# One wait per PE instruction in the sorted edge steps of a graph network

## The chip, the cores and the metric

The kernel runs on one core of one Trainium2 chip. The metric is the device time of the whole program in microseconds. The kernel before takes 2650.18 us, the median of 3 runs (2649.66 to 2650.37).

## The reference

Four message-passing steps on a graph with 3125 nodes of 128 features and 50000 edges, then a final layer norm over the sum with the input. The edges come sorted by their target node. All tensors are fp32.

```python
edge_attr = swish(edge_attr_raw @ enc_W + enc_b)              # 50000 x 4 -> 50000 x 128
for _ in range(4):
    e_in = concatenate([edge_attr, x[src], x[dst]], axis=-1)  # 50000 x 384
    e_upd = layernorm(swish(e_in @ eW1 + eb1) @ eW2 + eb2, eg, ebeta)   # hidden width 256
    edge_attr = edge_attr + e_upd
    agg = segment_sum(edge_attr, dst, num_segments=3125)
    n_in = concatenate([x, agg], axis=-1)
    x = x + layernorm(swish(n_in @ nW1 + nb1) @ nW2 + nb2, ng, nbeta)
x = layernorm(x_in + x)
```

## The kernel before

The program is written by hand, engine by engine: each engine has its own instruction list, and order between engines comes from counting semaphores (`wait_ge` in front of an instruction, `then_inc` on one). For sorted edges the class `Fast` is used.

The 50000 edges are cut into G1 = 98 groups of GE = 512 edges (TPG = 4 tiles of 128). One step s (0 to 3) runs over its 98 groups and then does the node update. Groups are counted on through the steps, n = 98 s to 98 s + 97. Features that need precision are kept as two fp16 parts, high and low, so most products are three matmuls.

In one iteration n PE does, in this order:

- `hidden(n)`, the first layer, into the PSUM tile `ps_h(n % 2)`: L1595, 4 matmuls of 256 columns, adds the target node's part by a one-hot matrix `oht` from a window of the node table (`q_win`, semaphores q0 to q3); L1603, 16 matmuls of 128 columns, adds the gathered source rows (`rows`, fetched by GpSimd's indirect DMAs); L1615, 6 matmuls of 512 columns, multiplies the old edge state by the weights and raises "h".
- `turn(n + 1)` (steps 1 to 3): L1629, 8 transposes of the next group's stored state, raises "transposed". ACT copies them (L1789) and raises "eT", for which L1615 of the next group waits.
- `output(n - 1)`, the second layer, into `ps_v`: L1642 puts the bias down (in step 0 from the third group on ACT's copy L1752, "seed", does this), then L1647, 24 matmuls of 128 columns, six for each tile t; raises "v". It waits for "hl", the low part of the hidden values, DVE's L1843.
- `turn_back(n - 4)` (step 0 alone): L1659, 8 matmuls.
- `node_sums(n - 7)`: in step 0 L1674, 4 matmuls, then L1678, 8 matmuls, which sum a group's edges into a window of 128 nodes in PSUM, `ps_a`; raises "sum". There is one `ps_a`, so it has to wait till DVE has added the window of the group before to `agg` (L1923, in step 0 L1920: "added"); it also waits for the group's new state ("el", DVE's L1904) and in step 0 for the one-hot matrix ("oh" of the init semaphores).
- `encode(n + 2)` (step 0 alone): L1384, one fp32 matmul that encodes the raw edge attributes.

ACT does for each group two swish passes over `ps_h` (L1743, L1744, 1024 columns), the copy L1789, four squares with sums (L1765), and the high part of the new state (L1779). DVE works in slots, one a group. Slot n is: the window add of group n - 8 ("added"), in step 0 the one-hot matrices of group n + 2 (L1475, L1476) and a low part (L1484), then L1843 of group n ("hl"), then a reciprocal root over pairs of groups (L297 to L305; seven to nine of its eleven small operations lie in odd slots, the rest in even ones), the scaling of group n - 4 (L1884, L1895), the low part of group n - 6 (L1904, "el"), and the gain L1853 of group n - 1 ("gu"). In odd slots L1904 comes behind the scaling, in even ones ahead of it.

SP loads the stored state (L1514, semaphores st0 to st7), the one-hot matrices (L1519, oh0 to oh3, which waits for "h" of group n - 4 and "sum" of group n - 12), stores the new state (L1532) and loads the window of the node table (L1526, L1527). GpSimd issues four gathers a group (L1572); the first waits for L1603 of group n - 4, the third for "v" of group n - 5.

Of the kernel before, what the change touches and what calls it, by code (L numbers as in the profile page):

```python
# [32 lines left out]
TPG = 4  # L33
GE = TPG * P
G1 = -(-E // GE)
# [9 lines left out]
R = 4  # L45
# [4 lines left out]
LAG = 4  # L50
# [12 lines left out]
def build_program(nc, attr_t, x_in, src_in, dst_in, attr_in, enc_W, enc_b, eW1, eb1, eW2, eb2, eg, ebeta,  # L63
                  nW1, nb1, nW2, nb2, ng, nbeta, out):
    ctx = ExitStack()
    with ctx:
# [1254 lines left out]
        class Fast:  # L1321
# [52 lines left out]
            def encodes(self, pe):  # L1374

                def encode(n):
                    if n >= G1:
                        return
                    pe.wait_ge(Z(f"at{n % R}"), 16 * self.ring(n))
                    if n == 1:  # L1380
                        pe.wait_ge(Z("enc"), n)
                    if n >= 4:
                        pe.wait_ge(self.S("gu"), n - 3)
                    pe.matmul(self.encoded(n), enc5[:, :], at5[n % R][0:RAW + 1, :],  # L1384
                              start=True, stop=True, skip_group_check=True).then_inc(Z("encm"), 1)

                return encode
# [189 lines left out]
            def pe(self, pe, s, node):  # L1577
# [3 lines left out]
                def hidden(n):  # L1581

                    k, k2 = n % R, n % 2
                    both_hot = oht[n % R12]
                    if s:
                        pe.wait_ge(S(f"oh{k}"), 16 * self.ring(n))
                    else:
                        pe.wait_ge(Z("oht"), n + 1)
                    pe.wait_ge(S(f"q{k}"), 32 * self.ring(n))
                    if n >= 2:  # L1590
                        pe.wait_ge(S("hl"), n - 1)
                    fence(pe)
                    for half in range(2):
                        for h in range(2):
                            pe.matmul(ps_h(k2)[:, half, h * HALF_E:(h + 1) * HALF_E],  # L1595
                                      q_win[k][:, h * H + half * D:h * H + half * D + D],
                                      both_hot[:, h * HALF_E:(h + 1) * HALF_E],
                                      start=h == 0, stop=False, skip_group_check=True)
                    pe.wait_ge(*self.gathered(n))
                    for t in range(TPG):  # L1600
                        for half in range(2):
                            for p in range(2):
                                x = pe.matmul(ps_h(k2)[:, half, t * P:(t + 1) * P],  # L1603
                                              rows[k][:, t, p * H + half * D:p * H + half * D + D], ident16[:, :],
                                              start=False, stop=False, skip_group_check=True)
                    x.then_inc(S("src"), 1)
                    if s:
                        pe.wait_ge(S("eT"), n - G1 + 1)
                    else:
                        pe.wait_ge(Z("lo"), n + 1)  # L1610
                    old = eT[k2] if s else turned_in[n % RE]
                    for half in range(2):
                        cols = slice(half * D, (half + 1) * D)
                        for w, p in ((w1_hi, 0), (w1_hi, 1), (w1_lo, 0)):
                            x = pe.matmul(ps_h(k2)[:, half, :], w[:, cols], old[:, p, :],  # L1615
                                          start=False, stop=w is w1_lo, skip_group_check=True)
                    x.then_inc(S("h"), 1)

                def turn(n):
# [1 line left out]
                    if not first <= n <= last or s == 0:  # L1621
                        return
                    pe.wait_ge(*self.loaded(n))
                    if n > G1:
                        pe.wait_ge(S("eT"), n - G1)
                    for p in range(2):
                        for t in range(TPG):
                            m = p * TPG + t
                            x = pe.transpose(ps_t[:, m * P:(m + 1) * P], st_in[n % RE][:, p, t * P:(t + 1) * P], ident16[:, :])  # L1629
                    x.then_inc(S("transposed"), 1)  # L1630

                def output(n):

                    k2 = n % 2
                    if s == 0 and n >= 2:
                        pe.wait_ge(S("seed"), n - 1)
                    else:
                        if n >= 2:
                            pe.wait_ge(S("gu"), n - 1)
                        if s == 0:  # L1640
# [1 line left out]
                        pe.matmul(ps_v(k2), ones16[:, :], v_bias[:, :], start=True, stop=False, skip_group_check=True)  # L1642
                    pe.wait_ge(S("hl"), n + 1)
                    for t in range(TPG):
                        for half in range(2):
                            for h, w in ((hh, w2_hi), (hh, w2_lo), (hl, w2_hi)):
                                x = pe.matmul(ps_v(k2)[:, t * P:(t + 1) * P], h[k2][:, half, t * P:(t + 1) * P], w[:, half, :],  # L1647
# [3 lines left out]
                def turn_back(n):  # L1651
# [3 lines left out]
                    if n:  # L1655
                        pe.wait_ge(S("new"), n)
                    for t in range(TPG):
                        for p in range(2):
                            x = pe.matmul(ps_e[:, t * P:(t + 1) * P], turned_in[n % RE][:, p, t * P:(t + 1) * P], ident16[:, :],  # L1659
                                          start=t == 0 and p == 0, stop=p == 1, skip_group_check=True)  # L1660
# [2 lines left out]
                def node_sums(n):  # L1663
# [1 line left out]
                    if n < first:  # L1665
                        return
                    pe.wait_ge(S("el"), n + 1)
                    if n:
                        pe.wait_ge(S("added"), n)
                    if s == 0:  # L1670
                        pe.wait_ge(Z("oh"), n + 1)
                    fence(pe)
                    for t in range(TPG if s == 0 else 0):
                        pe.matmul(ps_a[:, P:2 * P], ones16[:, :], oh[n % R12][:, t * P:(t + 1) * P],  # L1674
                                  start=t == 0, stop=t == TPG - 1, skip_group_check=True)
# [740 lines left out]
```

## Time and profile before

| | us |
|---|---|
| median of 3 runs | 2650.18 |
| the profiled execution, span | 3010.4 |
| step 0, first to last L1595 | 93.2 to 744.7 |
| steps 1, 2, 3, first to last L1595 | 843.9 to 1475.5, 1572.4 to 2202.8, 2299.6 to 2929.2 |
| PE busy | 2519.3 (84%) |
| DVE busy | 2296.5 (76%) |
| ACT busy | 1995.8 (66%) |
| POOL busy | 1569.8 (52%) |

The profiled execution's own span is 360 us longer than the median of the runs without a profile. Times in the rows are microseconds from the start of the span.
### The profile page before, as it was taken

The numbers are of one execution on the slowest core, as the hardware profiler recorded it, in microseconds if no ns is written. First come the engines' busy times: TensorE is split into PE (matmuls) and PEld (weight loads), VectorE is DVE, ScalarE is ACT, GpSimd is POOL, SyncE is SP. The second block draws the span as 40 slices with busy tenths as digits, with TensorE's granted clock in tenths as the row PEclk, the third lists the DMA queues.
The fourth block names the chain that finished last, engine by engine and source line by source line (L and its number), as shares of the span: only waits on it lengthen the run. The fifth ranks groups of instructions, "written<-read, shape, count | busy, mean of one in ns | idle before, by whom it ended". The sixth has DMA issues, their size and how long they took to land.

```text
span 3010.4 us, 83926 instructions
## 1 busy us (share of the span) xinstructions
PE 2519.3 (84%) x27990; PEld 1876.1 (62%) x27990; DVE 2296.5 (76%) x6586; ACT 1995.8 (66%) x5343; POOL 1569.8 (52%) x1581
## 2 busy tenths in 40 slices
PE   3699999999858888888876888888885888888885
PEld 1467776677536666666645666666663666666664
DVE  5499999899637787777854787777773688877787
ACT  2478787777437777777635777777753777777774
POOL 0566666664056666666215666666603666666640
PEclk9799999999989999999999999999998999999998
DMA  3556666564256666667445666666734555555540
GB/s 95 158 180 178 185 184 186 177 184 147 93 151 206 209 207 207 207 209 210 129 137 156 209 210 208 206 207 210 209 101 138 161 168 168 168 166 167 167 134 22
DMA packets 380881, 512.91 MB, mean 170 GB/s; under 512 B 57676, under 2 KB 254418, under 8 KB 380440
## 3 DMA queue, kind: packets, MB, share of 16 engines
q1 hardware_dynamic: 305176, 301.81, 32.0%
q0 software_dynamic: 75264, 205.62, 24.0%
q8 instruction: 228, 3.74, 0.5%
q14 instruction: 213, 1.74, 0.2%
HBM read 389.35 MB, written 117.85 MB: 168 GB/s over the span
## 4 chain that ended last, share of the span: by engine, by line
PE 76%; issue 11%; ACT 4%; another core or an unknown queue 4%; DVE 3%; DMA 1%; POOL 0%; DVEq 0%; ACTq 0%; SPq 0%; POOLq 0%
PE psum L1647 17%; PE psum L1615 16%; PE psum L1603 13%; PE psum L1678 6%; PE psum L1595 6%; PE psum L1629 4%; PE psum L1384 3%; PE psum L2081 3%; PE psum L1642 2%; PE psum L2120 2%; PE psum L2094 1%; PE psum L1659 1%; ACT arena L1765 1%; ACT psum L1744 1%
## 5 line engine op out<-in xcount | busy, mean ns | idle before, releaser
L1572 POOL DMA_INDIRECT arena<-node_tables,idx_all x1568 | 1567.2, 999 | 1345.2 <-remote 528.1
L1843 DVE SCALAR_TENSOR_TENSOR arena<-psum,arena 128x1024 f16<-128x1024 f32 x392 | 479.6, 1223 | 520.6 <-issue 370.9
L1743 ACT ACTIVATE arena<-psum 128x1024 f16<-128x1024 f32 x392 | 401.1, 1023 | 576.4 <-PE psum L1615 443.9
L1647 PE MATMUL psum<-w_hi,arena 128*128 128x128 f16 x6272 | 604.1, 219 | 37.5 <-ACT psum L1752 21.9
L1603 PE MATMUL psum<-ident,arena 128*128 128x128 f16 x6272 | 481.4, 220 | 165.9 <-issue 160.5
L1647 PE MATMUL psum<-w_lo,arena 128*128 128x128 f16 x3136 | 553.1, 219 | 3.8 <-issue 3.1
L1647 PEld LDWEIGHTS psum<-w_hi,arena 128*128 128x128 f16 x6272 | 498.2, 98 | 75.8 <-ACT psum L1752 40.3
L1603 PEld LDWEIGHTS psum<-ident,arena 128*128 128x128 f16 x6272 | 390.4, 98 | 242.1 <-issue 222.5
L1615 PE MATMUL psum<-arena,w_hi 128*128 128x512 f16 x1568 | 473.3, 384 | 41.3 <-ACT arena L1789 39.8
L1765 ACT ACTIVATE arena<-psum 128x128 f32<-128x128 f32 x1568 | 412.5, 279 | 100.9 <-remote 79.2
L1744 ACT ACTIVATE psum<-psum 128x1024 f32<-128x1024 f32 x392 | 398.9, 1018 | 0.0
L1884 DVE SCALAR_TENSOR_TENSOR arena<-arena 128x128 f32<-128x128 f32 x1176 | 366.8, 343 | 3.0
L1647 PEld LDWEIGHTS psum<-w_lo,arena 128*128 128x128 f16 x3136 | 307.0, 98 | 46.7 <-issue 5.6
L1765 ACT ACTIVATION_READ_ACCUMULATOR arena<-psum 128x1 f32 x1568 | 327.9, 209 | 0.0
L1789 ACT COPY arena<-psum 128x1024 f16<-128x1024 f16 x294 | 298.9, 1017 | 42.6 <-remote 38.3
L1678 PE MATMUL psum<-arena 128*128 128x128 fp8e4 x3136 | 241.6, 219 | 96.2 <-issue 87.9
L1615 PE MATMUL psum<-arena,w_lo 128*128 128x512 f16 x784 | 300.4, 383 | 0.0
L1853 DVE TENSOR_TENSOR arena<-psum,g_row 128x512 f32<-128x512 f32 x392 | 267.5, 682 | 9.9 <-ACT arena L1765 6.8
L1904 DVE SCALAR_TENSOR_TENSOR arena<-arena 128x512 f16<-128x512 f32 x392 | 267.8, 683 | 0.0
L1595 PE MATMUL psum<-arena 128*128 128x256 fp8e4 x1568 | 241.3, 275 | 31.4 <-issue 23.5
L1678 PEld LDWEIGHTS psum<-arena 128*128 128x128 f16 x3136 | 188.5, 98 | 126.6 <-issue 125.6
L1779 ACT CAST arena<-arena 128x512 f16<-128x512 f32 x392 | 248.7, 635 | 0.0
(174 smaller groups left out, 3258.7 us busy)
## 6 DMA issues: line engine op xcount, KB each, us to landing
state<-arena SPq DMA_DIRECT2D x294, 256.0 KB
arena<-state SPq DMA_DIRECT2D x294, 256.0 KB
arena<-node_tables SPq DMA_DIRECT2D x784, 64.0 KB
arena<-matrices SPq DMA_DIRECT2D x294, 128.0 KB
node_tables<-arena SPq DMA_DIRECT2D x100, 256.0 KB, 2.2
arena<-node_tables,idx_all POOLq DMA_INDIRECT x1568
arena<-rel_rows SPq DMA_DIRECT2D x98, 128.0 KB
matrices<-arena SPq DMA_DIRECT2D x98, 128.0 KB
```

What stands on the lines that cost most here:

```text
L1572: pool.indirect_dma_start(out=rows[n % R][:, t, :], out_offset=None, in_=p_table, in_offset=bass.IndirectOffsetOnAxis(ap=idx_all[:, n % G1 ...
L1595: pe.matmul(ps_h(k2)[:, half, h * HALF_E:(h + 1) * HALF_E], q_win[k][:, h * H + half * D:h * H + half * D + D], both_hot[:, h * HALF_E:(h ...
L1603: x = pe.matmul(ps_h(k2)[:, half, t * P:(t + 1) * P], rows[k][:, t, p * H + half * D:p * H + half * D + D], ident16[:, :], start=False, st ...
L1615: x = pe.matmul(ps_h(k2)[:, half, :], w[:, cols], old[:, p, :], start=False, stop=w is w1_lo, skip_group_check=True)
L1647: x = pe.matmul(ps_v(k2)[:, t * P:(t + 1) * P], h[k2][:, half, t * P:(t + 1) * P], w[:, half, :], start=False, stop=half == 1 and h is hl, ...
L1678: x = pe.matmul(ps_a[:, 0:P], st_out[n % R][:, p, t * P:(t + 1) * P], oh[n % R12][:, t * P:(t + 1) * P], start=t == 0 and p == 0, stop=t = ...
L1743: act.activation(hh[k2], ps_h(k2), ACT.Silu).then_inc(S("hh"), 1)
L1744: act.activation(ps_h(k2), ps_h(k2), ACT.Silu).then_inc(S("h32"), 1)
L1765: x = act.activation(sq[k2][:, t * P:(t + 1) * P], ps_v(k2)[:, t * P:(t + 1) * P], ACT.Square, accum_out=nv[pair][:, m:m + 1])
L1789: act.copy(eT[n % 2], ps_t[:, :].rearrange("c (k e) -> c k e", k=2)).then_inc(S("eT"), 1)
L1843: dve.scalar_tensor_tensor(hl[k2], ps_h(k2), 1.0, hh[k2], ALU.mult, ALU.subtract).then_inc(S("hl"), 1)
L1884: x = dve.scalar_tensor_tensor(e_new[k][:, cols], gu[k][:, cols], rs[pair][:, m:m + 1], old, ALU.mult, ALU.add)
```

## The change

Six places of `Fast`, all in what PE does in the edge steps:

- `hidden`: the fence is gone. The waits for the one-hot matrix (in steps 1 to 3 "oh k", in step 0 "oht") and for "hl" of group n - 2 in front of L1595 are gone; only the window's wait "q k" stays (in step 0 "oht" for the first two groups). In step 0 from the fourth group on, the second half of L1615 waits for "seed" of the group whose output follows.
- `turn`: its wait for "eT" is gone. Before its fifth transpose it now waits for the one-hot matrix "oh" of the group that it turns.
- `output`: in step 0 "seed" is waited for here only at the last group; before tile t = 1 stands the wait for "oht" of the group after next (step 0), and before tile t = 3, the last, the wait for "added", with the same count for which `node_sums` of the same iteration waited. It stands from the eighth group of a step on.
- `turn_back`: before t = 2 stands the wait for the raw attributes that the `encode` of this iteration reads.
- `node_sums`: the fence is gone and so is "oh"; "added" is waited for here only at the step's edges (its first group and its last ones).
- `encode`: waits for its attributes itself only for the first six groups.

```diff
-                    pe.wait_ge(Z(f"at{n % R}"), 16 * self.ring(n))
+                    if n < LAG + 2:
+                        pe.wait_ge(Z(f"at{n % R}"), 16 * self.ring(n))
...
-                    if s:
-                        pe.wait_ge(S(f"oh{k}"), 16 * self.ring(n))
-                    else:
+                    if s == 0 and n < 2:
                         pe.wait_ge(Z("oht"), n + 1)
                     pe.wait_ge(S(f"q{k}"), 32 * self.ring(n))
-                    if n >= 2:
-                        pe.wait_ge(S("hl"), n - 1)
-                    fence(pe)
...
                         cols = slice(half * D, (half + 1) * D)
+                        if half and s == 0 and n >= 3:
+                            pe.wait_ge(S("seed"), n - 2)
...
-                    if n > G1:
-                        pe.wait_ge(S("eT"), n - G1)
                     for p in range(2):
+                        if p:
+                            pe.wait_ge(S(f"oh{n % R}"), 16 * self.ring(n))
...
-                    if s == 0 and n >= 2:
+                    if s == 0 and n == last:
                         pe.wait_ge(S("seed"), n - 1)
-                    else:
+                    if s or n < 2:
...
                     for t in range(TPG):
+                        if t == 1 and s == 0 and n + 2 <= last:
+                            pe.wait_ge(Z("oht"), n + 3)
+                        if t == TPG - 1 and n - 6 > first:
+                            pe.wait_ge(S("added"), n - 6)
...
                     for t in range(TPG):
+                        if t == 2 and n + LAG + 2 < G1:
+                            pe.wait_ge(Z(f"at{(n + LAG + 2) % R}"), 16 * self.ring(n + LAG + 2))
...
                     pe.wait_ge(S("el"), n + 1)
-                    if n:
+                    if n == first and n or n + 6 > last:
                         pe.wait_ge(S("added"), n)
-                    if s == 0:
-                        pe.wait_ge(Z("oh"), n + 1)
-                    fence(pe)
```

## Rows read from the trace of the kernel before

**Rows 1.** The page: busy time of each engine, and the chain that ended last.
```profile
PE 2519.3 (84%) x27990; PEld 1876.1 (62%) x27990; DVE 2296.5 (76%) x6586; ACT 1995.8 (66%) x5343; POOL 1569.8 (52%) x1581
...
PE 76%; issue 11%; ACT 4%; another core or an unknown queue 4%; DVE 3%; DMA 1%; POOL 0%; DVEq 0%; ACTq 0%; SPq 0%; POOLq 0%
```

**Rows 2.** Line L1595, steps 0 and 1: ns min/median/max, first and last start.
```profile
L1595 PE MATMUL psum<-arena x392: 272/273/421, 93.2 to 744.7; 128*128 128x256 fp8e4 x196
L1595 PE MATMUL psum<-arena x392: 269/273/417, 843.9 to 1475.5; 128*128 128x256 fp8e4 x196
```

**Rows 3.** Groups of PE instructions, step 1: busy us, mean ns | idle before.
```profile
L1603 PE MATMUL psum<-ident,arena 128*128 128x128 f16 x1552 | 123.9, 220 | 53.8 <-issue 53.6
...
L1678 PE MATMUL psum<-arena 128*128 128x128 fp8e4 x717 | 55.5, 218 | 26.5 <-issue 26.5
```

**Rows 4.** Timeline in the middle of step 1: L1615's end and ACT's L1743.
```profile
1117.89 0.38 PE L1615 MATMUL psum<-arena,w_lo 128*128 128x512 f16 x1
1119.63 1.02 ACT L1743 ACTIVATE arena<-psum 128x1024 f16<-128x1024 f32 x1 [1.55 <-PE psum L1615]
```

**Rows 5.** Timeline of the last groups of step 1.
```profile
1464.33 0.60 PE L1595 MATMUL psum<-arena 128*128 128x256 fp8e4 x4
...
1467.62 0.22 PE L1647 MATMUL psum<-w_hi,arena 128*128 128x128 f16 x1
...
1468.90 0.22 PE L1647 MATMUL psum<-w_hi,arena 128*128 128x128 f16 x1
...
1469.10 0.28 DVE L1923 TENSOR_TENSOR agg_deg<-agg_deg,psum 128x128 f32 x1
1469.30 1.22 DVE L1843 SCALAR_TENSOR_TENSOR arena<-psum,arena 128x1024 f16<-128x1024 f32 x1
1469.48 0.61 PE L1678 MATMUL psum<-arena 128*128 128x128 fp8e4 x8 [0.36 <-issue]
1469.92 0.60 PE L1595 MATMUL psum<-arena 128*128 128x256 fp8e4 x4
...
1472.33 0.38 PE L1615 MATMUL psum<-arena,w_lo 128*128 128x512 f16 x1
...
1472.75 1.02 ACT L1743 ACTIVATE arena<-psum 128x1024 f16<-128x1024 f32 x1 [1.17 <-PE psum L1615]
...
1474.39 0.28 DVE L1923 TENSOR_TENSOR agg_deg<-agg_deg,psum 128x128 f32 x1
...
1474.49 0.22 PE L1647 MATMUL psum<-w_hi,arena 128*128 128x128 f16 x1
...
1474.77 0.61 PE L1678 MATMUL psum<-arena 128*128 128x128 fp8e4 x8
1474.77 1.22 DVE L1843 SCALAR_TENSOR_TENSOR arena<-psum,arena 128x1024 f16<-128x1024 f32 x1
1475.21 0.60 PE L1595 MATMUL psum<-arena 128*128 128x256 fp8e4 x4
```

**Rows 6.** The fences on PE's sequencer, whole run: ns min/median/max, starts.
```profile
L288 PEldq EVENT_SEMAPHORE  x784: 51/51/6122, 93.1 to 2966.3; - x196
```

**Rows 7.** Timeline in the middle of step 0: L1595, and DVE's window add.
```profile
305.18 0.61 PE L1595 MATMUL psum<-arena 128*128 128x256 fp8e4 x4
311.89 0.61 PE L1595 MATMUL psum<-arena 128*128 128x256 fp8e4 x4
318.13 0.61 PE L1595 MATMUL psum<-arena 128*128 128x256 fp8e4 x4
...
308.38 0.41 DVE L1920 TENSOR_TENSOR agg_deg<-agg_deg,psum 128x256 f32 x1
```

**Rows 8.** Step 0: the seed, L1647 behind it; then all its waits in sum.
```profile
307.64 0.59 ACT L1752 COPY psum<-v_row 128x512 f32<-128x512 f32 x1
...
308.28 0.23 PE L1647 MATMUL psum<-w_hi,arena 128*128 128x128 f16 x1 [0.30 <-ACT psum L1752]
...
PE psum L1647 <- ACT psum L1752: 21.9, 24, 1.8
```

## The prediction

> **What bounds the kernel now.** I read the page first: the engine with most busy time is PE, 84% of the span, and the chain that ended last runs over PE for 76% of it [rows 1]. Then the time by stage: the loop over the groups takes 651.5 us in step 0 and 631.6 us in step 1 [rows 2], and within 2 us of that in steps 2 and 3. In step 1 that is 631.6 / 97 = 6.51 us a group, while PE's own work for a group, from L1678 at 1469.48 to the end of L1647 (last start 1474.49, free again at 1474.55), is 5.07 us without a gap [rows 5].
>
> The profiled run is 360 us longer than the median of 2650.18 us, so first it must be known what the recording adds. In mid-loop ACT starts L1743 at 1119.63, although the last L1615 matmul that it waits for is shown from 1117.89 to 1118.27: 1.36 us late [rows 4]. In the last groups of step 1 the same handover takes 0.04 us (1472.33 + 0.38 to 1472.75), and the groups take 5.59 and 5.29 us (L1595 at 1464.33, 1469.92, 1475.21) [rows 5]. In mid-loop PE also idles inside L1603, where no line waits: 53.6 us of "issue" in step 1 [rows 3]; the last two groups have none of it. I take these two groups as the kernel without the recording's load. The Trainium skill (Perfetto Trace Analysis, Tensor Engine Instruction) says that the end shown for a matmul is an estimate and that the semaphore's propagation is not in the record; the trace agrees in so far as an increment can come well behind the end shown.
>
> The check on that choice: with 5.44 instead of 6.51 us, the 291 groups of steps 1 to 3 lose 311 us; with 6.24 us in step 0, which PE fills without a gap from 311.89 to 318.13, instead of 651.5 / 97 = 6.72 [rows 2, 7], another 46 us go. 3010.4 - 311 - 46 = 2653 us, against 2650.18 measured.
>
> So what makes a group 5.44 us when PE's work is 5.07? In [rows 5] PE is through with L1647 at 1468.96 and starts L1678 only at 1469.48; DVE's window add L1923 ends at 1469.38. In the next group L1923 ends at 1474.67 and L1678 starts at 1474.77. Both times it is 0.10 us behind the add. So "added" releases PE, and not "el", which L1904 raises earlier in the same slot of DVE. From the add it is a loop over three engines: 0.10 us, L1678 to the end of L1615 (1469.48 to 1472.71), ACT's L1743 and L1744, DVE's L1843 at 1474.77: 5.39 us after the add's end. DVE needs 5.37 us from L1843 to the end of its next window add in this slot, an odd one (1469.30 to 1474.67); even slots are shorter. Two groups therefore take at least 5.39 + 5.37 = 10.76 us, 5.38 us each. That is what binds, not PE's 5.07 us.
>
> **The change part by part.** *Standalone waits.* A fence or a second wait is an instruction of PE's sequencer, 51 ns when it doesn't block [rows 6]; four a group go in steps 1 to 3, six in step 0. Those behind L1678 have its 0.44 us and the matmuls of L1595 as cover, the one of `turn` has L1603: 0. Without any cover it would be 4 x 0.051 x 294 + 6 x 0.051 x 98 = 90 us. The fence in front of L1678 is different: there the matmul starts 0.10 us behind the add. A wait attached to the weight load takes 0.05 us: ACT's L1752 ends at 308.23, L1647 starts at 308.28 [rows 8]. That is a gain of 0.05 us on the loop.
>
> *The covered waits*, "hl" of group n-2 in `hidden` and "eT" in `turn`: PE's queue has already waited for both values, in `output` and `hidden`. 0.
>
> *"added"* moves from in front of L1678 to t = 3 of `output`. The count is the same, but six L1647 matmuls now stand behind it. L1647 repeats every (1468.90 - 1467.62) / 23 = 0.056 us, so 6 x 0.056 = 0.33 us of PE's work moves from before the add's end to behind it. Is PE held there? t = 3 would start at 1467.62 + 18 x 0.056 = 1468.63 and at 1474.49 - 5 x 0.056 = 1474.21, against add ends of 1469.38 and 1474.67: held for 0.75 and 0.46 us, so all of the 0.33 us goes onto the loop [rows 5]. Queued behind it are the rest of `output`, for which ACT's squares wait (they stand behind L1744 and L1789 in ACT's list, and that is their cover), then `node_sums` and `hidden` and through it ACT and DVE. Bounds: 0 if the add were always early, the 0.33 us in every group if the loop were one slot long.
>
> *"oh"* moves to the middle of `turn(n+1)`, some 2.4 us ahead of its old place. The load waits for L1615 of four groups before, so about three groups less 2.4 us remain to it, 13 us; nothing in the rows shows PE waiting for it. 0.
>
> *"seed"* in step 0 moves ahead of the second half of L1615, three matmuls or 0.65 us earlier. L1647 is held by it 24 times, 21.9 us in sum [rows 8]. In the recorded run its new place would come at 305.18 + 0.44 + 0.89 + 0.65 = 307.16, before the seed's end at 308.23 [rows 7, 8]; that lateness is of the size of the recording's 1.36 us, so without it the seed is about in time: 0, with an upper bound of 24 x 0.65 = 16 us. *"oht", "at"*: nothing waits for them in the rows, 0. *"added"* in step 0: L1920 ends at 308.79, and PE is at t = 3 only at 308.28 + 1.01 = 309.29: 0 [rows 7, 8].
>
> **The sum.** On the loop +0.33 - 0.05 = +0.28 us for two groups, 0.14 us each: 5.52 instead of 5.38. It acts where the new wait exists and a later `hidden` follows it: 89 groups in each of three steps, 267. 267 x 0.14 = 37 us. On the profiled execution cleared of the recording that is 2653 + 37 = 2690, on the median 2650 + 37 = 2687 us. I forecast 2687, 1.4% slower. The profiled span won't show this: in mid-loop the recording holds it, and four to six records of some 140 a group go, so it may even fall (2940 to 3030 us).
>
> **The rivals.**
> A, the forecast: the "added" loop binds. For it: 0.10 us behind the add in both undisturbed groups, and the check of 2653 us. Against: only two groups a step show it. Its price lies between +18 us (half the groups held) and 0.33 x 267 = +89 us.
> B, faster: what costs is that the sequencer stands in the fence while PE's queue runs dry; with every wait attached it reads on. The Trainium skill (Advanced Engine Details and Errata, Sequencer Loop) says this much, that an engine instruction waits in the queue while later ones are read. From rows: the idle time before L1678 is 0.36 us in one undisturbed group and 1474.77 - 1474.55 = 0.22 us in the next [rows 5]; were it the fence's own, 0.29 x 294 = 85 us would go, and all standalone instructions exposed give 90 us: 2560. A half of it is 2605. For it: 26.5 us of "issue" before L1678 in step 1 [rows 3]. Against: that idle time ends 0.10 us behind L1923, which an attached wait sits out too.
> C, the same: in the run without a profile most groups are uneven, as step 0's 6.71 beside 6.24 us [rows 7], and the earlier wait meets an add already done: 2645 to 2655.
> D, slower in another place: the seed holds L1615 in step 0 and so delays `hidden` itself, up to +16 us, beside A.
>
> **How the numbers follow.** A, with D on top, 0.60 (2668 to 2740, mostly under 2715); B 0.22 (2560 to 2644); C 0.18. About 0.2%, 5 us, is what a measurement of this kernel can tell from no change. Faster 0.22, same 0.17, slower 0.61. A's own range is 2668 to 2715; to leave out no more than 2 in 10 it takes in C and the nearer half of B: 2610 to 2715.
>
> **What would show it.** In the profile of the changed kernel: no rows of L288, L1591 or L1625 on PE inside the loops. In the last two groups of a step the idle time sits inside L1647, ahead of its last six matmuls, and ends 0.05 us behind L1923; L1678 follows without a gap, and the L1595 distances are 0.1 to 0.3 us longer than 5.59 and 5.29. For B they would be about 5.1 to 5.2 us. The forecast is wrong if in undisturbed groups the add ends before PE is at t = 3, or if the idle time at L1603 is in the unprofiled run too and not only in the record.

## The result and the profile after

The changed kernel takes 2712.89 us, the median of 4 runs (2710.74 to 2717.46), beside 2649.92 us for the kernel before in the same rounds. The ratio is 1.0241, 95% interval [1.0228, 1.0253]: 63 us slower, where 37 were forecast.

The page of after, the rows that answer to [rows 1]:
```profile
PE 2428.5 (90%) x27990; PEld 1868.7 (69%) x27990; DVE 2289.2 (84%) x6586; ACT 1983.8 (73%) x5343; POOL 1627.4 (60%) x1581
```
The span of this profiled execution is 2711.4 us, what the runs take without a profile, so nothing has to be cleared away. The shares of busy time went up although the kernel got slower, because the span of before was stretched by 360 us. Its busy microseconds are stretched too: PE has the same 27990 matmuls in both and 2519.3 us there against 2428.5 here. So neither can be compared with [rows 1].

The line that was L1595 is L1591 now, in steps 0 and 1, as [rows 2]:
```profile
L1591 PE MATMUL psum<-arena x392: 272/273/418, 93.4 to 702.7; 128*128 128x256 fp8e4 x196
...
L1591 PE MATMUL psum<-arena x392: 272/273/422, 805.1 to 1347.5; 128*128 128x256 fp8e4 x196
```
Step 1 takes 542.4 us, 5.59 us a group. I had taken 5.44 us for before, and to its loop of 5.38 us the forecast added 0.14 to get 5.52. (These rows run to the last of the last group's four matmuls; to its first it is 542.1 us, as in the table below.)

Groups of PE instructions in step 1 (busy us, mean ns | idle before), as [rows 3]; L1649 is the old L1647, L1679 the old L1678:
```profile
L1649 PE MATMUL psum<-w_hi,arena 128*128 128x128 f16 x1536 | 153.0, 220 | 37.8 <-DVE agg_deg L1924 37.5
...
L1599 PE MATMUL psum<-ident,arena 128*128 128x128 f16 x1552 | 103.4, 220 | 3.7 <-DMA arena<-node_tables,idx_all 3.7
...
L1679 PE MATMUL psum<-arena 128*128 128x128 fp8e4 x717 | 54.7, 219 | 0.0
```
The idle time has left the window sums and sits inside the second layer, and what ends it is the window add. L1599, the old L1603, has lost its 53.6 us of "issue".

Timeline of the last groups of step 1, as [rows 5]:
```profile
1335.01 0.28 DVE L1924 TENSOR_TENSOR agg_deg<-agg_deg,psum 128x128 f32 x1
...
1335.34 0.23 PE L1649 MATMUL psum<-w_hi,arena 128*128 128x128 f16 x1 [0.85 <-DVE agg_deg L1924]
...
1335.69 0.61 PE L1679 MATMUL psum<-arena 128*128 128x128 fp8e4 x8
1336.13 0.60 PE L1591 MATMUL psum<-arena 128*128 128x256 fp8e4 x4
...
1338.55 0.38 PE L1613 MATMUL psum<-arena,w_lo 128*128 128x512 f16 x1
1338.96 1.02 ACT L1744 ACTIVATE arena<-psum 128x1024 f16<-128x1024 f32 x1 [1.42 <-PE psum L1613]
...
1341.00 1.23 DVE L1844 SCALAR_TENSOR_TENSOR arena<-psum,arena 128x1024 f16<-128x1024 f32 x1 [1.13 <-issue]
1341.21 0.60 PE L1591 MATMUL psum<-arena 128*128 128x256 fp8e4 x4
...
1346.10 0.27 DVE L1924 TENSOR_TENSOR agg_deg<-agg_deg,psum 128x128 f32 x1
...
1347.22 0.60 PE L1591 MATMUL psum<-arena 128*128 128x256 fp8e4 x4
```
The loop of the forecast can be followed row by row. The add ends at 1335.29, the held matmul starts 0.05 us later, six matmuls pass before L1679 at 1335.69, L1613 ends at 1338.93, ACT takes over at 1338.96, L1844 starts at 1341.00, 5.71 us behind the add, and the next long slot's add ends at 1346.37, 5.37 us later. The group distances are 5.08 and 6.01 us, 11.09 for two, where [rows 5] have 5.59 and 5.29. One group in two isn't held at all: the six matmuls add to every second group, as the two-slot loop has it. The sign that I had named, both distances 0.1 to 0.3 us longer than 5.59 and 5.29, was too narrow: one is shorter, and only the sum of the two is longer.

In mid-loop the slot on DVE is a little longer:
```profile
1005.57 1.22 DVE L1844 SCALAR_TENSOR_TENSOR arena<-psum,arena 128x1024 f16<-128x1024 f32 x1 [1.06 <-issue]
1006.71 0.23 DVE L297 TENSOR_SCALAR arena<-arena 128x8 f32<-128x8 f32 x1
...
1010.74 0.28 DVE L1924 TENSOR_TENSOR agg_deg<-agg_deg,psum 128x128 f32 x1
...
1011.07 0.23 PE L1649 MATMUL psum<-w_hi,arena 128*128 128x128 f16 x1 [0.84 <-DVE agg_deg L1924]
```
From L1844 to the add's end are 5.45 us here (1011.02 - 1005.57), and 5.46 as the median of the long slots of steps 1 to 3. With 5.71 that gives 11.17 us for two groups, the measured 5.59 each. Nearly all of the 0.08 us more than at the step's end is in one operation, L297, the root's first, which takes 0.16 us there (at 1342.14) and 0.23 here.

### The profile page after: what moved, and what is told of

Its sections match the earlier page's. It is cut to its first block, busy times and chain, and to the rows that moved or that the text cites. A ratio compares the mean times of both kernels' runs of the same rounds, so it can differ in the third digit from the quotient of the medians.

```text
span 2711.4 us, 82205 instructions
## 1 busy us (share of the span) xinstructions
PE 2428.5 (90%) x27990; PEld 1868.7 (69%) x27990; DVE 2289.2 (84%) x6586; ACT 1983.8 (73%) x5343; POOL 1627.4 (60%) x1581
## 4 chain that ended last, share of the span: by engine, by line
PE 68%; issue 11%; DVE 8%; ACT 7%; POOL 3%; DMA 2%; DVEq 1%; ACTq 0%; SPq 0%; POOLq 0%
PE psum L1613 17%; PE psum L1649 12%; PE psum L1599 12%; PE psum L1679 6%; PE psum L1591 6%; ACT psum L1745 5%; PE psum L1385 4%; POOL arena L1573 3%; PE psum L2082 2%; PE psum L2121 2%; PE psum L1627 2%; DVE agg_deg L1924 2%; PE psum L1663 2%; PE psum L2095 2%; DVE arena L1885 1%
## 5 line engine op out<-in xcount | busy, mean ns | idle before, releaser
L1573 POOL DMA_INDIRECT arena<-node_tables,idx_all x1568 | 1624.8, 1036 | 985.1 <-DMA node_tables<-arena 421.2
L1649 PE MATMUL psum<-w_hi,arena 128*128 128x128 f16 x6272 | 624.2, 220 | 129.6 <-DVE agg_deg L1924 119.7
L1844 DVE SCALAR_TENSOR_TENSOR arena<-psum,arena 128x1024 f16<-128x1024 f32 x392 | 478.3, 1220 | 236.2 <-issue 138.6
L1649 PEld LDWEIGHTS psum<-w_hi,arena 128*128 128x128 f16 x6272 | 502.1, 98 | 175.6 <-DVE agg_deg L1924 147.5
L1649 PE MATMUL psum<-w_lo,arena 128*128 128x128 f16 x3136 | 556.9, 220 | 0.0
L1613 PE MATMUL psum<-arena,w_hi 128*128 128x512 f16 x1568 | 470.4, 382 | 1.3 <-ACT arena L1790 1.3
L1599 PE MATMUL psum<-ident,arena 128*128 128x128 f16 x6272 | 417.8, 220 | 14.4 <-DMA arena<-node_tables,idx_all 14.3
L1599 PEld LDWEIGHTS psum<-ident,arena 128*128 128x128 f16 x6272 | 384.5, 98 | 28.5 <-DMA arena<-node_tables,idx_all 19.6
L1766 ACT ACTIVATION_READ_ACCUMULATOR arena<-psum 128x1 f32 x1568 | 339.3, 216 | 0.0
L1649 PEld LDWEIGHTS psum<-w_lo,arena 128*128 128x128 f16 x3136 | 307.2, 98 | 45.8
L1613 PE MATMUL psum<-arena,w_lo 128*128 128x512 f16 x784 | 299.3, 382 | 0.0
L1591 PE MATMUL psum<-arena 128*128 128x256 fp8e4 x1568 | 238.6, 275 | 26.0 <-DMA arena<-node_tables 26.0
L1679 PE MATMUL psum<-arena 128*128 128x128 fp8e4 x3136 | 240.9, 220 | 5.9 <-DVE agg_deg L1924 5.9
L1896 DVE SCALAR_TENSOR_TENSOR arena<-arena 128x512 f32<-128x512 f32 x294 | 205.2, 698 | 5.1
```

The costliest lines, as they stand in the source:

```text
L1573: pool.indirect_dma_start(out=rows[n % R][:, t, :], out_offset=None, in_=p_table, in_offset=bass.IndirectOffsetOnAxis(ap=idx_all[:, n % G1 ...
L1591: pe.matmul(ps_h(k2)[:, half, h * HALF_E:(h + 1) * HALF_E], q_win[k][:, h * H + half * D:h * H + half * D + D], both_hot[:, h * HALF_E:(h ...
L1599: x = pe.matmul(ps_h(k2)[:, half, t * P:(t + 1) * P], rows[k][:, t, p * H + half * D:p * H + half * D + D], ident16[:, :], start=False, st ...
L1679: x = pe.matmul(ps_a[:, 0:P], st_out[n % R][:, p, t * P:(t + 1) * P], oh[n % R12][:, t * P:(t + 1) * P], start=t == 0 and p == 0, stop=t = ...
L1766: x = act.activation(sq[k2][:, t * P:(t + 1) * P], ps_v(k2)[:, t * P:(t + 1) * P], ACT.Square, accum_out=nv[pair][:, m:m + 1])
L1844: dve.scalar_tensor_tensor(hl[k2], ps_h(k2), 1.0, hh[k2], ALU.mult, ALU.subtract).then_inc(S("hl"), 1)
```

## The experiments

Times are medians; the ratio is to the kernel before in the same rounds (2653.2 us for the first four, 2647.6 for e5 to e8, 2650.8 for the last four). "Step 1" is from the first group's first matmul of L1595 to the last group's. "Release" is the median time from an add's end to the matmul that it holds, and "to low" from the add's end to the L1843 that hangs on it, both over steps 1 to 3 of the trace; where the early adds scatter it (e6, e9 to e12), "to low" is the tenth percentile.

| kernel | us | ratio [95%] | step 1 | a group | release | to low |
|---|---|---|---|---|---|---|
| after | 2712.9 | 1.0241 [1.0228, 1.0253] | 542.1 | 5.59 | 0.057 | 5.71 |
| e1_added_back | 2658.9 | 1.0028 [1.0017, 1.0039] | 528.9 | 5.45 | 0.147 | 5.45 |
| e2_added_alone | 2719.2 | 1.0251 [1.0234, 1.0268] | 542.3 | 5.59 | 0.057 | 5.71 |
| e3_no_fence | 2663.5 | 1.0038 [1.0024, 1.0052] | 529.2 | 5.46 | 0.146 | 5.45 |
| e4_seed_back | 2715.2 | 1.0236 [1.0219, 1.0253] | 542.0 | 5.59 | 0.057 | 5.71 |
| e5_added_t1 | 2836.1 | 1.0708 [1.0690, 1.0725] | 573.9 | 5.92 | 0.057 | 6.38 |
| e6_early_add_before | 2625.8 | 0.9910 [0.9893, 0.9926] | 517.3 | 5.33 | 0.101 | 5.40 |
| e7_early_add_after | 2670.6 | 1.0080 [1.0063, 1.0097] | 530.1 | 5.47 | 0.057 | 5.71 |
| e8_added_only | 2645.8 | 0.9991 [0.9981, 1.0001] | 524.5 | 5.41 | 0.058 | 5.38 |
| e9_added_only_early | 2622.4 | 0.9893 [0.9876, 0.9909] | 515.0 | 5.31 | 0.057 | 5.37 |
| e10_load_first | 2626.2 | 0.9904 [0.9888, 0.9921] | 519.5 | 5.36 | 0.102 | 5.41 |
| e11_load_first_added_only | 2627.2 | 0.9911 [0.9894, 0.9927] | 518.7 | 5.35 | 0.058 | 5.38 |
| e12_short_gain | 2625.1 | 0.9908 [0.9892, 0.9925] | 519.3 | 5.35 | 0.102 | 5.41 |

**e1_added_back**: the changed kernel with "added" waited for in `node_sums` again.
```diff
-                        if t == TPG - 1 and n - 6 > first:
-                            pe.wait_ge(S("added"), n - 6)
...
-                    if n == first and n or n + 6 > last:
+                    if n:
                         pe.wait_ge(S("added"), n)
```

> The changed kernel with one thing undone: the wait for added stands in front of L1678's matmuls again, at every group, and no longer at t = 3 of output. All else stays as changed: no fences, seed, oh, oht and at at their new places. Theory L (the loop DVE window add, PE, ACT, DVE binds, and the six second-layer matmuls behind the moved wait are what was added to it): all or nearly all of the 63 us go back, 2645 to 2658 us. Rival S (a good part comes from seed in step 0, or from the other moved waits): 2665 us or more. Rival F (the fences did some good, for instance by holding PE's sequencer back): stays near 2700.

Measured 2658.9 us, 1 us above the expected upper end: 54 of the 63 us are back by this wait alone. All else of the change stays in, without the gain that rival B gave it; it is even 0.28% slower than before.

**e2_added_alone**: the mirror of it, the kernel before with its fences and only this wait moved.
```diff
+                        if t == TPG - 1 and n - 6 > first:
+                            pe.wait_ge(S("added"), n - 6)
...
-                    if n:
+                    if n == first and n or n + 6 > last:
                         pe.wait_ge(S("added"), n)
```

> The kernel before with one part of the change alone: added is waited for at t = 3 of output instead of in the fence of node_sums. Both fences and every other wait stay as before. Theory L: the loop gets the 0.33 us and keeps the fence's other waits, 2695 to 2715 us. Rivals S and F: the move alone costs at most a third of the 63 us, under 2672.

Measured 2719.2 us, 4 above the expected upper end: the whole loss and a little more, with the same step of 542.3 us. The place of one wait is shown to be the cause, by putting it in and by taking it out.

**e3_no_fence**: before, without fences and covered waits; "added" stays in `node_sums`, behind "el".
```diff
-                    if n >= 2:
-                        pe.wait_ge(S("hl"), n - 1)
-                    fence(pe)
...
-                    if n > G1:
-                        pe.wait_ge(S("eT"), n - G1)
...
-                    if n:
-                        pe.wait_ge(S("added"), n)
                     if s == 0:
                         pe.wait_ge(Z("oh"), n + 1)
-                    fence(pe)
+                    if n:
+                        pe.wait_ge(S("added"), n)
```

> The kernel before without the two fence increments and without the two covered waits (hl in hidden, eT in turn); all other waits stay where they were, so a second wait is still an instruction of its own. Theory L: standalone instructions are covered and an attached added is some 0.05 us quicker over a loop of two groups, so 2640 to 2650 us. Were the standalone instructions worth their 51 ns each on PE (2 fences, 1 or 2 waits a group), 2600 to 2620. On the record: if the fences are what makes the profiled execution of the kernel before 360 us longer than its unprofiled time, this one's span is within 30 us of its time; if it is the number of recorded instructions, it stays above 2900.

Measured 2663.5 us, 10 slower and not up to 10 faster: a miss. The timeline of a held group, and the line of the waits of `node_sums` (L1666) on PE's sequencer:
```profile
1107.65 0.28 DVE L1917 TENSOR_TENSOR agg_deg<-agg_deg,psum 128x128 f32 x1
...
1108.05 0.46 PEld L1672 LDWEIGHTS psum<-arena 128*128 128x128 f16 x8 [0.72 <-issue]
1108.08 0.61 PE L1672 MATMUL psum<-arena 128*128 128x128 fp8e4 x8 [0.58 <-DVE agg_deg L1917]
```
```profile
L1666 PEldq EVENT_SEMAPHORE  x391: 51/51/51, 144.7 to 2619.7; - x196
```
The matmul starts 0.15 us behind the add's end, where the fence of before needs 0.10 [rows 5]. 0.046 us more on a loop of two groups is 0.023 a group; over the 264 groups of steps 1 to 3 in which "added" is waited for that is 6 us, more than half of the 10.

**e4_seed_back**: the changed kernel with "seed" waited for in `output` again.
```diff
-                        if half and s == 0 and n >= 3:
-                            pe.wait_ge(S("seed"), n - 2)
...
-                    if s == 0 and n == last:
+                    if s == 0 and n >= 2:
                         pe.wait_ge(S("seed"), n - 1)
```

> The changed kernel with the seed wait of step 0 back in output, in front of the second layer, instead of ahead of the second half of L1613. Theory L: seed is in time at either place, 2708 to 2716 us. Rival S: up to 16 us of the 63 are its, 2697 to 2705.

Measured 2715.2 us beside 2712.9: step 0 takes 611.4 us with it back and 609.0 without. Its ratio and after's lie within each other's intervals. Moving the seed costs nothing that can be measured; rival D's addition is out.

**e5_added_t1**: three times the dose. "added" stands before t = 1, 18 matmuls ahead of the end and not 6; "oht" changes places with it.
```diff
-                        if t == 1 and s == 0 and n + 2 <= last:
+                        if t == TPG - 1 and s == 0 and n + 2 <= last:
                             pe.wait_ge(Z("oht"), n + 3)
-                        if t == TPG - 1 and n - 6 > first:
+                        if t == 1 and n - 6 > first:
                             pe.wait_ge(S("added"), n - 6)
```

> The changed kernel with added waited for at t = 1 of output instead of t = 3 (oht in step 0 goes to t = 3 in exchange): eighteen second-layer matmuls stand behind the wait instead of six, 0.67 us more of PE's work. Theory L: the loop of two groups grows from 11.17 to 11.84 us, 5.92 us a group, over 267 groups +89 us on 2713: 2790 to 2815 us. Were the 63 us a cost of having a wait in the middle of output at all (a bubble at the wait), and not of what stands behind it, it would stay at 2705 to 2725.

Measured 2836.1 us, 21 above the expected upper end. PE's waits, the first for steps 1 to 3, the second for step 0 (us, times, longest):
```profile
PE psum L1649 <- DVE agg_deg L1924: 218.9, 159, 3.6
PE psum L1649 <- DVE agg_deg L1921: 27.0, 46, 3.3
```
"To low" goes from 5.71 to 6.38 us, 0.67 for 12 matmuls, 0.056 each, exactly the price of the forecast. The loops of steps 1 to 3 take 98 us more than after's together, which alone would be inside the expected range. In 132 pairs of groups the matmuls make 88 of them, and L297, 0.30 us here and 0.25 in after (medians), some 7. The other 25 us come from step 0, 634.2 us beside 609.0, where the add holds PE more often and longer than in after.

**e8_added_only**: e1 with "el" waited for only at a step's first group, so that "added" is the only wait and stands on the load.
```diff
-                    pe.wait_ge(S("el"), n + 1)
+                    if n == first:
+                        pe.wait_ge(S("el"), n + 1)
```

> The changed kernel with added back in front of L1678, as in the first of these experiments, and without the wait for el wherever added covers it (DVE raises el of group n in an earlier slot than the added that node_sums(n) waits for). So added is the only wait there and stands on the weight load itself. In the first experiment it stood on an instruction of the sequencer and L1678 began 0.147 us behind the add, against 0.101 behind the fence of the kernel before and 0.057 where it stands on the load at t = 3. Theory L with that delay as a term of the loop: 0.05 to 0.09 us less on a loop of two groups than there, 2645 to 2653 us. If the delay does not matter, the same as there, 2656 to 2662.

Measured 2645.8 us, in the expected range. In a held group:
```profile
962.62 0.28 DVE L1923 TENSOR_TENSOR agg_deg<-agg_deg,psum 128x128 f32 x1
...
962.95 0.62 PE L1678 MATMUL psum<-arena 128*128 128x128 fp8e4 x8 [0.43 <-DVE agg_deg L1923]
```
0.05 us behind the add. This is what the change could have been: one wait per instruction, without moving "added". It ends within 0.1% of before, so the 0.04 us saved against the fence is hardly to be seen, and it is some 10 us better than e1 (by the ratios, 0.9991 and 1.0028). Its loop closes in mid-loop too: 5.375 us to the low part and 5.38 to the end of the next long slot's add are 10.755 us, and the pairs of groups in steps 1 to 3 take 10.75 to 10.76 (median).

**e6_early_add_before** and **e7_early_add_after**: the remedy that the loop suggests, on either kernel. DVE does the window add ahead of the gain and not behind it. The same edit in both:
```diff
+                def early_add(m):
+                    if first <= m < last - 6:
+                        add_window(m, window(m))
...
-                    add_window(n - LAG - 4, window(n - LAG - 4))
+                    if n - LAG - 4 >= last - 6:
+                        add_window(n - LAG - 4, window(n - LAG - 4))
...
+                        early_add(n - LAG - 3)
                         gains(n - 1)
```

> The kernel before with DVE's window add moved ahead of the gain L1853 of the slot before (0.60 us earlier in DVE's list; the last seven groups of a step as before). PE's list is untouched, fences included. Theory L: the loop of two groups shrinks from 10.84 to 10.24 us, 5.12 us a group, where PE's own 5.07 us is nearly reached: -0.30 us over some 280 groups, 2560 to 2580 us. If the loop over added is not what binds the kernel before, nothing moves: 2645 to 2655.

> The changed kernel with the same earlier window add on DVE. Theory L: the loop shrinks from 11.17 to 10.57 us, 5.28 us a group, so 80 to 90 us below 2713: 2620 to 2640 us, slower than the same edit on the kernel before by about the same 50 to 60 us. If the change's cost were elsewhere on PE, the edit would give much less here than on the kernel before.

Measured 2625.8 and 2670.6 us: 22 and 42 us gained, right in direction, and well short of both expected ranges. DVE in a long slot of e6:
```profile
964.59 0.16 DVE L301 TENSOR_TENSOR arena<-arena 128x8 f32<-128x8 f32 x1
964.91 0.29 DVE L1923 TENSOR_TENSOR agg_deg<-agg_deg,psum 128x128 f32 x1 [0.16 <-issue]
965.11 0.68 DVE L1853 TENSOR_TENSOR arena<-psum,g_row 128x512 f32<-128x512 f32 x1
965.71 1.21 DVE L1843 SCALAR_TENSOR_TENSOR arena<-psum,arena 128x1024 f16<-128x1024 f32 x1
```
And the window from 850 to 1300 us (busy us of PE, its loads, DVE, ACT and POOL, then clock, DMA share, GB/s):
```profile
850.00:1300.00 450.00, 438.32 (x5694) 357.32 (x5692) 428.98 (x1230) 375.41 (x1018) 345.15 (x345) 1.00 0.82 250
```
The add came only 0.35 to 0.41 us earlier (5.08 instead of 5.43 us behind L1843 in long slots, 4.30 instead of 4.71 in short ones) and not the whole length of the gain: 0.16 us of idle time stands in front of it now. Two more things can be read here. DVE goes from L1853 to L1843 without a gap, and it is busy for 428.98 of the 450 us. So there were two theories for the missing gain: X, the loop from the add still binds; Y, DVE is full. The last four runs were made for that.

**e9_added_only_early**: e8's waits with the early add.

> The kernel of e8_added_only (no fences, no standalone waits in the loop, added attached to the first weight load of the window sums) with DVE's window add ahead of the gain, as in e6_early_add_before. e6 took 2625.8 us and not the 2570 expected; two reasons are in question. X: the loop from the add over PE and ACT to the low part still binds, 5.40 us behind the add plus 5.1 to 5.2 us on DVE to the add of the long slot, 5.25 to 5.30 us a group. Y: DVE itself is full (in the middle of step 1 of e6 it is busy 429 of 450 us). By X the shorter release here (5.38 instead of 5.40 us) brings 0.01 to 0.02 us a group, 3 to 5 us: 2620 to 2624. By Y it brings nothing: 2623 to 2628. This run alone won't tell them apart; it says whether the one-wait form and the early add go together.

Measured 2622.4 us, ratio 0.9893 [0.9876, 0.9909], where X expected 2620 to 2624. This is the shortest time of the study. It is below before beyond doubt, but the 3 us to e6 are within the spread of either (2619.6 to 2624.2 beside 2621.6 to 2627.1), and Y's 2623 to 2628 begins 1 us above: as expected, this run doesn't tell X from Y. The traces do: the median pair of groups takes 10.43 us in step 1 of e9 (5.375 to low and 5.05 on DVE) and 10.50 in e6 (5.40 and 5.08), so in most groups the add's loop binds.

**e12_short_gain**: e6 with half of the gain left out.
```diff
+                    T = TPG if n < LAG else 2
...
-                                      g_row[:, :].unsqueeze(1).to_broadcast([P, TPG, D]), ALU.mult).then_inc(S("gu"), 1)
+                                      g_row[:, :].unsqueeze(1).to_broadcast([P, T, D]), ALU.mult).then_inc(S("gu"), 1)
```

> e6_early_add_before with half of DVE's gain left out from the fifth group on (256 instead of 512 elements), a part of the computation that is missing in the result: 0.3 us less work of DVE a slot, behind the add and ahead of the next low part, so not on the add's loop. X (the add's loop binds) expects next to nothing: 2618 to 2626. Y (DVE is full) expects the group to fall from 5.33 to about 5.1 us, 50 to 70 us in all: 2560 to 2578.

Measured 2625.1 us, the time of e6 with 78 us less work on DVE (2225.2 instead of 2303.6 us busy). Y doesn't hold for the loop as a whole: DVE had idle time now (20.4 us ahead of L1843 from 850 to 1300 us), and no group got shorter by it. But that the time is the same is in part luck, since two things cancel. The first row is from e12, the second from e6:
```profile
959.04 0.35 DVE L297 TENSOR_SCALAR arena<-arena 128x8 f32<-128x8 f32 x1
```
```profile
895.61 0.82 DVE L2218 TENSOR_TENSOR x_all<-x_all,nbeta_row 128x640 f32<-128x640 f32 x1
```
L297 takes 0.35 us in e12 and 0.16 in e6, and it lies on the add's loop: the long slot takes 5.23 us instead of 5.08, and the median pair 10.64 instead of 10.50. In e6, on the other hand, DVE has one more operation, L2218 (`shift`, 0.82 us), in five slots of a step and one of its kind in five more of step 3. It stands between the gain and L1843 and puts that off, and one group behind it takes about 6.04 us and not 5.43: five times in steps 1 and 2, ten times in step 3. In e12, where the gain is shorter, no group at these places does. So here Y holds, for some 12 us of e6.

**e10_load_first**: e6 with the register load at the head of the slot.
```diff
+                held = {}
...
-                        add_window(m, window(m))
+                        add_window(m, held.pop(m))
...
+                    if first <= n - LAG - 3 < last - 6:
+                        held[n - LAG - 3] = window(n - LAG - 3)
```

> e6_early_add_before with one difference: the register that holds the window's column is loaded at the head of DVE's slot and not right in front of the add. In e6 the add of a long slot stands 0.16 us behind the last small operation of the root, with no wait that holds it; if that is the register load, the idle time goes. By X and by Y alike two groups get shorter by up to 0.16 us (X) or 0.33 us (Y, both slots), 0.08 to 0.16 us a group, 24 to 48 us in 291 groups: 2580 to 2603 us. If the 0.16 us is something else, the time stays at e6's 2625.

Measured 2626.2 us, no gain. PE's waits from 850 to 1300 us, in e6 and then in e10:
```profile
PE psum L1678 <- DVE agg_deg L1923: 5.2, 8, 0.8
PE psum L1678 <- issue: 4.7, 24, 0.3
PE psum L1603 <- DMA arena<-node_tables,idx_all: 0.3, 1, 0.3
```
```profile
PE psum L1603 <- DMA arena<-node_tables,idx_all: 12.1, 21, 1.5
PE psum L1678 <- DVE agg_deg L1923: 0.4, 2, 0.2
```
The edit did what it was made for: the idle time in front of the add is gone (L1904 at 961.62 and L1923 at 962.29 follow closely), and PE's wait for the add falls from 9.9 us to 0.4. Its place is taken at once by L1603, which waits for the gathered source rows, 12.1 us instead of 0.3. These rows count idle time only from the shown end of a matmul, 0.22 us behind its start. From start to start, over what the same two lines take when nothing holds them, PE lost 18.5 us in this window in e6, in 46 of 85 groups and all of it ahead of L1678; in e10 it lost 4.1 us there and 17.1 ahead of L1603. So neither X nor Y is the answer for e10; the gathers are the next limit, and they lie within a few microseconds of the add's.

**e11_load_first_added_only**: e10's DVE order with e8's waits.

> e10_load_first's order on DVE together with e8_added_only's waits on PE. By X 3 to 5 us below e10: 2576 to 2599. By Y, and if by then PE's own 5.07 us come near, the same as e10.

Measured 2627.2 us, the same as e10 and 5 us above e9. With the gathers in the lead a shorter release buys nothing. Over the whole run its L1599 (the old L1603) waits 60.4 us in 71 places, e9's 19.7 in 19.

What holds the gathers back is open. GpSimd is busy for 347 of the 450 us of that window in e10, the DMA engines for 0.83 of it, and its first gather of a group waits for L1603 of four groups before; no run separates these. A second window buffer for the sums, which might take the add off PE's path, wasn't tried: the program's tiles already use all eight parts of its PSUM tensor.

## Why the prediction came out as it did

Its direction and its mechanism were right, the size was 26 us short. The range holds the result by 2 us only, in part by luck: the 26 us are three terms that I had put at nothing.

**What bounds the kernel: right.** The two groups at a step's end were the kernel without the recording's load. e1, e3 and e8, whose records aren't stretched and which differ from before only in how PE waits, take 5.41 to 5.46 us a group beside the 5.44 assumed. e5 and e2 move the time through the "added" wait alone.

**The price of six matmuls: right.** 5.71 us from add to low against e8's 5.38, with the same 0.057 us of release: 0.33 us, as forecast. e5 gives the same 0.056 us a matmul for twelve more.

**Attached instead of fence: right in size.** 0.101 to 0.057 us, forecast 0.10 to 0.05. It takes effect only where nothing else stands beside it; with "el" still in front (e1, e3) the release grew to 0.147 us, and I hadn't priced that.

**DVE's part of the loop: a term put at nothing.** I had taken DVE's 5.37 us, read from one slot at a step's end, to be the same before and after. In e8, whose time is that of before, it is 5.38 in mid-loop, so as a base it was good. In after it is 5.46, in e5 5.52, and nearly all of the difference is L297. Its median is 0.16 us in before, e1, e3, e6 and e8 to e11, where "added" stands in front of L1678, 0.25 to 0.26 in after, e2 and e4 and 0.32 in e7, where it stands at t = 3, and 0.30 in e5. The place of the wait alone doesn't set it, for in e12 it is 0.35. Two groups therefore grow by 0.33 - 0.04 + 0.08 = 0.37 us and not by 0.28. The count of groups was right: the first nine distances of a step take as long in after as in e8 (5.53 and 5.51 us on average), the other 88 take 5.60 and 5.40. 264 x 0.185 = 49 us stand beside the 37 forecast. Why L297 gets longer stays open: GpSimd's gathers, which are silent at the step's end, are there in e8's mid-loop as well, and its L297 stays at 0.16.

**Two more terms forecast at nothing: they weren't.** After against e8: steps 1 to 3 take 53 us more, step 0 609.0 instead of 601.9, and all that lies outside the four loops 475.7 instead of 468.1 us. 53 + 7 + 8 = 68 is the whole difference of their spans (2711.4 - 2643.6). Of the 53, up to 6 are the release, by which e8 is quicker than before. The other two can be read in after's record, the first row of what L1649 waits for in step 0 (us, times), the second from the end of step 1:
```profile
  DVE agg_deg L1921: 6.8, 30
```
```profile
1357.51 0.29 PE L1649 MATMUL psum<-w_hi,arena 128*128 128x128 f16 x1 [2.97 <-DVE agg_deg L1924]
```
In step 0 I had argued that PE reaches t = 3 half a microsecond behind the add. On the stretched record that was so, but here the add holds L1649 30 times, 6.8 us in sum, and e8 has no such wait. At a step's end the last group's second layer is held too: PE starts its last matmul 10.8 us behind the last group's L1591 and not 7.4 as in e8, at the end of steps 1 to 3, and 11.2 instead of 8.2 in step 0. How much of these 3.0 to 3.4 us reaches the next step differs (0.4 to 3.1 us). e2 has the same 610.9 and 477.2 us, so both terms belong to "added".

**Covered waits, fences, "oh", "seed", "oht", "at" at 0: right**, as far as e1, e4 and e8 show them together. The standalone instructions had their cover.

**Rival B fell.** Fences gone and "added" in its place (e1, e3, e8) is between 0.1% faster and 0.4% slower, not 1.7 to 3.4% faster. The idle time before L1678 was not the fence's. The Trainium skill (Advanced Engine Details and Errata, Sequencer Loop) is not contradicted: instructions may well be queued behind a waiting one, though no row here shows the reading ahead itself. It just was not what ended the idle time; DVE's add did, 0.1 us before each start. **Rival C fell** as well: in after's record, which isn't stretched, the groups do alternate, 5.07 and about 6.10 us, but with the add late in one of two and not in few.

**The profiled span: wrong.** I forecast 2940 to 3030 us; it was 2711.4. I had taken the stretching for a property of the kernel under a profile, and it belonged to that one execution. All thirteen other profiled executions lie within 3 us of their own unprofiled counterparts, e2 and e6 with the fences and the 27990 matmuls of before among them. The sign that I named was the idle time at L1603, 53.6 us of "issue" in step 1: in all of them no "issue" is left there, and the line's idle time is 4 to 7 us (18 in e10 and e11), put down to the gathers.

## What to carry to other kernels

A wait costs more the earlier it stands: every instruction between the new place and the old one goes onto the loop that the wait closes, here six matmuls, 0.33 us, in every second group. Before a wait is moved "to where there is room for it", find who raises it and when; if the engine already idles for it, leave it where it is and drop or cover the other conditions instead (e8), or make the raiser earlier (e6, e9). A loop's length is to be taken from many of its turns in the middle of a kernel's own record, and a change can lengthen an instruction that it doesn't touch (L297 here); if the span of a profiled run isn't the unprofiled time, its total must not be taken as the base for the next kernel.

## What the runs showed of the hardware

The time from the end of DVE's add to PE's start depends on where the wait stands, with almost no scatter: 0.057 us when it is the only condition and attached to the weight load (some 155 to 160 held groups of steps 1 to 3 each in after, e2 and e8, tenth to ninetieth percentile within 0.002), 0.101 us when it ends a standalone sequencer instruction in front of a load without a condition (144 in e6), and 0.147 us when a load with a condition of its own, raised earlier, follows the standalone instruction (some 160 each in e1 and e3). Which of two waits becomes the attached one isn't given by their order in the source (e3).

The same small DVE instruction, L297 on 128x8 elements, takes 0.16 us as a median in e8, 0.25 in after, 0.30 in e5 and 0.35 in e12, with nothing changed in it. No run separates what lengthens it.

One profiled execution of fourteen was 360 us, 14%, longer than the kernel, with ACT starting late behind the shown end of the matmul that it waits for: 1.36 us in [rows 4], 1.26 as the median of the 392 handovers from L1615 to L1743, where after, e6 and e8 have 0.04. Neither the fences nor the number of records explains it, and its cause stays open.
